# A graph-and-experts kernel: operands of the last diffusion step formed ahead, its last tiles written out apart, the expert pass unrolled

## The chip, the core and the metric

One core of one Trainium2 chip runs the whole program. The metric is the device time of one execution in microseconds (us). The kernel before takes 1402.74 us (median of 3 runs, 1402.63 to 1402.93).

## The reference

The input is `x` (3125 x 256, float32) and a graph with 103,125 directed edges. The part that matters:

```python
h = silu(layernorm(x) @ W_in.T + b_in)          # 3125 x 256
term = out = h
for i in range(1, 7):                           # 6 diffusion steps
    term = segment_sum(term[src], dst) * inv_deg[:, None] / i
    out = out + term
x = x + out @ W_out.T + b_out
xn = layernorm(x) * gamma + beta                # second part: 8 experts, top 2
top_vals, top_idx = top_k(xn @ Wr + br, 2);  w = softmax(top_vals)
y = sum over e of w_e * (gelu(xn @ W1[e] + b1[e]) @ W2[e] + b2[e])   # W1[e] 256 x 512, W2[e] 512 x 256
x = x + y
```

## The kernel before, in words

The 3125 nodes are 25 tiles of 125 rows (T = 25, D = 256), in 5 groups of 5 (WIN = 5, NB = 5). The graph is held in SBUF as dense fp16 counts (`adj`, 25 x 25 blocks of 125 x 125). Since W_out is linear, it is applied first: `h_dram` holds silu(...) @ W_out.T, and each of the 6 steps forms `v = h + (adj v) * cinv` (a nested form of the sum). A vector is carried as two fp16 parts side by side (512 columns), in `v_a` and `v_b` by turns, so that a tile of a step is 25 matmuls of 125 x 512 into one PSUM bank.

Building `adj` and the first step take until about 330 us. **Steps 1 to 4** (`step`, 25 tiles each) follow. For each tile TensorE (L1552) makes the product; ScalarE (L750) evicts the high half to `t_hi`; VectorE adds the low half (L993, `psum_read`), adds the row of `h` that SyncE has put into the two-deep `h_ring` (L1000, `h_used`), splits the sum into high and low fp16 and stores them (L1009, L1011, `v_ready`). Five PSUM banks let TensorE run up to five tiles ahead of the eviction; a new step reads every tile of the last one. In groups 0 to 3 of each of these steps SyncE also loads one piece of the expert weights per tile (`w_piece`, 128 x 256, 64 pieces in all) and VectorE takes its largest absolute value (L1079).

**The last step** (`last_step` with a `body(i, u, has)` on every engine) runs one software pipeline: in the body of tile m stand, on VectorE, the router logits of tile m - 8, `x1 = v * scale + (x + b_out)` and the mean and variance of tile m - 1 (L1189 to L1195), once in five tiles the square roots of a group (`sd2`, `newton`), the second normalisation of tile m - 5 (L1212, L1215, `z_ok`), the low half of the expert input of tile m - 6 (L1220), and the eviction of tile m (L1235, L1242). GpSimd adds `b_out` to the loaded `x` rows (L637) and `beta` to the normalised rows (L640). ScalarE makes the high half of the expert input of tile m - 5 (L808), then evicts tile m (L813), then copies the transposed rows of tile m - 6 (L818). TensorE follows tile m with two transposes of tile m - 6 (L1608) and the router matmuls of tile m - 7 (L1617). It has three PSUM banks in a ring for the product. Groups 0 and 1 are written out, 2 to 4 are a loop, and two more written-out groups (`peeled(NB)`, `peeled(NB + 1)`) drain the pipeline. After tile 4 stand the power-of-two scales (`scales`), which need the weights' maxima through two all-reduces on GpSimd.

As the last step frees groups of `adj`, 16 weight matrices of 512 KB are loaded into them from ScalarE's queue (`PART_RAW`), multiplied by their scale and split into a high fp16 part by ScalarE (L797) and a low one by VectorE (L1230), one in each of the bodies u = 1 to 4 of i = 1 to 4.

**Then** VectorE makes the routing (top 2, positions, tile tables; L1252 to L1385) and **the expert pass** runs over FT = 56 tiles of 128 rows (`ffn_tiles`): GpSimd gathers the rows (L661) and scatters the results (L667), TensorE transposes the rows of tile j + 2 (L1643), multiplies tile j by W1 (L1658) and tile j - 3 by W2 (L1675), ScalarE does gelu (L854), VectorE the rest (L1396, L1405, L1407, L1415). It is 7 groups of FU = 8 tiles, the first and last written out, five in a loop; at the start of a group each engine loads the 8 table values that its instructions need as addresses (which expert, which part of `adj`): TensorE 2 such loads, VectorE 3, ScalarE 1 (L375). The combination of the two results per row and the store end the program.

## Time and profile before

| | us |
|---|---|
| median of 3 runs | 1402.74 |
| the profiled execution, its own time | 1399.97 |
| its span, first to last instruction | 1398.2 |
| TensorE busy (mean granted clock 0.927) | 1199.9 |
| VectorE busy | 744.3 |
| ScalarE busy | 364.5 |
| GpSimd busy | 167.7 |

Start and duration of instructions are in us from the start of the span. A clock of 1.00 is TensorE's full speed. Names such as L1598 are lines of the kernel before.

### The profile page before, as it was taken

The page shows a single profiled execution, that of the slowest core. Times are in us where ns is not written, and L with a number is a line of the kernel's source. Part 1 is how long each engine was busy: PE and PEld are TensorE (multiplying, and loading weights), DVE is VectorE, ACT ScalarE, POOL GpSimd, SP SyncE. Part 2 cuts the span into 40 slices and gives each one's busy share as a digit, 9 for nine tenths or more (in the row PEclk, how much of TensorE's full clock was granted, in tenths as well). Part 3 has the DMA queues.
Part 4 walks back from the last instruction along what each step waited for, and adds up shares of the span by engine and source line. Part 5 has one row for each costly group of instructions (what it writes and reads, how often), then busy time and mean ns, then how long its engine had stood idle before and what let it go on. Part 6 is the DMA issues. An engine that isn't in the chain of part 4 may idle for free.

```text
span 1398.2 us, 28001 instructions
## 1 busy us (share of the span) xinstructions
PE 1199.9 (86%) x7796; PEld 836.1 (60%) x7797; DVE 744.3 (53%) x1521; ACT 364.5 (26%) x706; POOL 167.7 (12%) x193
## 2 busy tenths in 40 slices
PE   4896999999999999999999999988885468778860
PEld 2784776665666666666666665545453357667750
DVE  7588999963333333333333333366566744554445
ACT  0574656640000000000000000022213223433423
POOL 2000000000000000000000000111111134555440
PEclk8897999999999999999999999999987579989995
DMA  5110010022111111111101110233332012112119
GB/s 155 30 52 19 23 38 29 29 84 57 41 44 37 38 40 45 33 35 44 46 27 45 41 46 22 51 106 102 101 109 76 17 50 65 62 61 64 58 45 269
DMA packets 65272, 81.72 MB, mean 58 GB/s; under 512 B 10997, under 2 KB 55981, under 8 KB 65085
## 3 DMA queue, kind: packets, MB, share of 16 engines
q1 hardware_dynamic: 49126, 49.55, 12.4%
q10 hardware_dynamic: 9908, 16.37, 4.2%
q0 software_dynamic: 6176, 15.01, 3.5%
q8 instruction: 35, 0.57, 0.2%
q14 instruction: 27, 0.22, 0.0%
HBM read 62.34 MB, written 19.50 MB: 59 GB/s over the span
## 4 chain that ended last, share of the span: by engine, by line
PE 63%; DVE 11%; DMA 9%; issue 8%; DVEq 3%; ACT 2%; POOL 1%; another core or an unknown queue 1%; ACTq 1%; SPq 0%; POOLq 0%
PE ps L1552 39%; PE ps L1530 7%; PE ps L1498 4%; PE ps L1658 3%; PE ps L1675 3%; DVE v_b L986 2%; DMA adj<-L_ffn_W 2%; DMA v_b<-xs_dram,v_a 2%; PE ps L1466 2%; DMA adj<-y_dram 2%; PE ps L1598 2%; PE ps L1477 1%; DMA v_a<-x 1%; DVEq L375 1%
## 5 line engine op out<-in xcount | busy, mean ns | idle before, releaser
L1552 PE MATMUL ps<-v_a,adj 125*125 125x512 f16 x1375 | 297.3, 379 | 0.0
L1552 PE MATMUL ps<-v_b,adj 125*125 125x512 f16 x1250 | 270.2, 379 | 2.2 <-DVE v_b L1011 2.2
L1552 PEld LDWEIGHTS ps<-v_a,adj 125*125 (+1 forms) x1375 | 187.6, 136 | 109.0
L1552 PEld LDWEIGHTS ps<-v_b,adj 125*125 x1250 | 170.6, 136 | 101.6 <-issue 2.6
L993 DVE SCALAR_TENSOR_TENSOR t_hi<-ps,cinv,t_hi 125x256 f32<-125x256 f32 x125 | 60.3, 482 | 284.2 <-ACT t_hi L750 284.2
L750 ACT ACTIVATE t_hi<-ps,cinv 125x256 f32<-125x256 f32 x125 | 59.4, 475 | 526.0 <-PE ps L1552 496.3
L986 DVE TENSOR_TENSOR v_b<-v_b 125x2560 f16<-125x2560 f16 x125 | 180.3, 1485 | 7.1 <-PE ps L1498 6.5
L1598 PE MATMUL ps<-v_b,adj 125*125 125x512 f16 x625 | 153.6, 409 | 5.5 <-DVEq L1128 3.4
L1675 PE MATMUL ps<-adj,v_b 128*128 x672 | 115.3, 283 | 25.5 <-issue 19.0
L727 ACT ACTIVATE adj<-ps 125x625 f32 (+1 forms) x125 | 111.8, 906 | 75.1 <-PE ps L1498 74.3
L1598 PEld LDWEIGHTS ps<-v_b,adj 125*125 (+1 forms) x625 | 90.5, 147 | 61.5 <-issue 13.1
L1658 PE MATMUL ps<-v_b,adj 128*128 128x128 f16 x1344 | 119.7, 228 | 5.6 <-issue 4.9
L854 ACT ACTIVATE v_b<-ps,v_a 128x128 f32<-128x128 f32 x224 | 84.2, 457 | 150.6 <-PE ps L1658 101.0
L1530 PE MATMUL ps<-v_a,adj 125*125 125x512 f16 x500 | 123.4, 380 | 0.0
L1498 PE MATMUL ps<-v_b 125*128 125x125 f16 x1250 | 95.8, 225 | 17.0 <-issue 9.4
L1498 PEld LDWEIGHTS ps<-v_b 125*128 125x128 f16 x1250 | 82.9, 100 | 42.1 <-DVE v_b L986 16.2
L1658 PEld LDWEIGHTS ps<-v_b,adj 128*128 x1344 | 97.9, 102 | 13.2 <-issue 7.1
L618 POOL MEMSET v_a<- 128x128 f32 x1 | 0.2, 205 | 843.9 <-DVEq L1128 843.9
L1000 DVE SCALAR_TENSOR_TENSOR t_hi<-h_ring,scale,t_hi 125x256 f32<-125x256 f32 x125 | 60.6, 484 | 33.4 <-issue 17.4
L1675 PEld LDWEIGHTS ps<-adj,v_b 128*128 128x128 f16 x672 | 57.4, 101 | 33.9 <-issue 27.6
L1530 PEld LDWEIGHTS ps<-v_a,adj 125*125 (+1 forms) x500 | 60.9, 136 | 25.6 <-issue 0.6
L667 POOL DMA_INDIRECT y_dram<-adj,v_a x56 | 57.7, 1030 | 103.5 <-DVE adj L1415 82.9
(230 smaller groups left out, 940.1 us busy)
## 6 DMA issues: line engine op xcount, KB each, us to landing
h_ring<-h_dram SPq DMA_DIRECT2D x150, 125.0 KB
w_piece<-L_ffn_W SPq DMA_DIRECT2D x64, 128.0 KB, 2.1
adj<-L_ffn_W ACTq DMA_DIRECT2D x16, 512.0 KB, 6.1
v_a<-x SPq DMA_DIRECT2D x25, 125.0 KB
xs_dram<-v_a SPq DMA_DIRECT2D x25, 125.0 KB
adj<-x ACTq DMA_DIRECT2D x5, 560.0 KB
adj<-y_dram SPq DMA_DIRECT2D x5, 560.0 KB
adj<-y_dram ACTq DMA_DIRECT2D x5, 560.0 KB
```

The costliest lines, as they stand in the source:

```text
L727: a.activation(adj_w[:, row, :, bass.ds(T * i + WIN * u, WIN)].rearrange("b o q p -> b (o q) p"), cells.rearrange("b c q -> b q c"), ACT.C ...
L750: a.activation(t_hi[0:NP, :], ps[0:NP, bank, 0:D], ACT.Copy, scale=cinv[0:NP, s, bass.ds(WIN * i + u, 1)]).then_inc(S["hi_ok"], 1)
L854: last = a.activation(h_g[r][:, b * 128:(b + 1) * 128], ps[:, 2 + r, b * 128:(b + 1) * 128], ACT.Gelu, bias=b1T[:, bass.ds(e * HK + b, 1)] ...
L986: v.tensor_tensor(one_hot_bq[RB[u]], iota_x[:, None, :, :].broadcast_to(pairs), mine[:, :, None, :].broadcast_to(pairs), ALU.is_equal).the ...
L993: v.scalar_tensor_tensor(t_hi[0:NP, :], ps[0:NP, bank, D:2 * D], cinv[0:NP, s, bass.ds(t, 1)], t_hi[0:NP, :], ALU.mult, ALU.add).then_inc( ...
L1000: v.scalar_tensor_tensor(t_hi[0:NP, :], h_ring[0:NP, u % 2, :], scale[0:NP, 0:1], t_hi[0:NP, :], ALU.mult, ALU.add).then_inc(S["h_used"], 1)
L1498: last = te.matmul(cells[:, j * 128:j * 128 + Q], one_hot_bq[RB[u]][:, j, :, k], one_hot_bq[RB[u]][:, WIN + j, 0:Q, k], start=(k == 0), st ...
L1530: last = te.matmul(ps[0:NP, early_bank(w), :], of_tile(adj[0:NP, 0:ADJ], r - 1, w, a * NP, NP), va[:, a, :], start=(a == 0), stop=(a == T ...
L1552: last = te.matmul(ps[0:NP, u, :], of_tile(adj[0:NP, 0:ADJ], i, u, a * NP, NP), source[:, a, :], start=(a == 0), stop=(a == T - 1))
L1598: last = te.matmul(ps[0:NP, RB[u], :], of_tile(adj[0:NP, 0:ADJ], i, u, a * NP, NP), vb[:, a, :], start=(a == 0), stop=(a == T - 1))
L1658: last = te.matmul(ps[:, 2 + r, b * 128:(b + 1) * 128], w_block(part1, low, at, 128), xT16[u % XR][:, part * DK + k, :], start=(n == 0 and ...
L1675: last = te.matmul(ps[:, 4 + r, 0:D], hp[u % FR][:, b, :], w_block(part2, low, b * D, D), start=(b == 0 and n == 0), stop=(b == HK - 1 and ...
```

## The change

- **Rows.** A new tensor `hx_dram` holds h + x + b_out. GpSimd writes it after the reduction of the weights' maxima: a DRAM-to-DRAM copy of `h_dram`, an accumulating DMA of `x`, and one of `b_out` broadcast over 3125 rows, each waited for (3.2 MB each). The last step loads its ring rows from it, and its second VectorE operation writes `x1` directly. The 25 loads of `x`, the GpSimd additions of `b_out` and the extra `x1` operation are gone.
- **Weights.** Steps 1 and 2 take the maxima over 32 halves of 128 x 512 (16 a step, in the part of the destination vector that tiles 20 to 24 will fill). After step 2 GpSimd reduces them and VectorE forms the scales. Steps 3 and 4 load each half again, ScalarE makes the high part, VectorE the low part, and SyncE stores both to `w16_dram`. The last step only loads the finished 512 KB per matrix, on SyncE's queue.
- **Order.** The square roots of tiles 0 to 3, 4 to 8, ..., 19 to 23 are taken at u = 4; tile 24 has its own. `xn2` and `xs_r` have five buffers instead of three, the transposed rows and their PSUM banks two instead of one. `peeled(NB)` and `peeled(NB + 1)` are replaced by a written-out piece on each engine.
- **Expert pass.** `ffn_tiles` is written out over all 56 tiles. Each engine loads one value per table and tile, for the next tile: TensorE 1 (`part_of`; the layer is now in a static base address), VectorE 2, ScalarE 1.

```diff
...
+            pool.wait_ge(S["w_top_ok"], 1)
+            g.partition_all_reduce(w_all, w_top, 128, bass.bass_isa.ReduceOp.max).then_inc(S["w_all_ok"], 1)
...
+            g.dma_start(hx_dram, h_dram).then_inc(S["hx_ok"], 16)
+            pool.wait_ge(S["hx_ok"], 16)
+            g.dma_start(hx_dram, x, max_dma_last_dim=8192, accum_op=ALU.add).then_inc(S["hx_ok"], 16)
+            pool.wait_ge(S["hx_ok"], 32)
+            g.dma_start(hx_dram, bass.AP(b_out.tensor, 0, [[0, N], [1, D]]), accum_op=ALU.add).then_inc(S["hx_ok"], 16)
...
             def step(s, t0, t1):
+                raw, lo16 = w_spare(step_dest(s))
+                if s > 0:
+                    sp.wait_ge(S["tile_ps"], s * T)
+
+                def store(i, u):
+
+                    sp.wait_ge(S["piece_used"], (s - 1) * NE // 2 * WP + i * WP + (u + 3))
+                    sp.dma_start(w16_half(s, i, u, 0), w_hi16[:, :]).then_inc(S["w16_out"], 16)
+                    sp.dma_start(w16_half(s, i, u, 1), lo16).then_inc(S["w16_out"], 16)
...
+                        if pieces and s > 2 and u < WP:
+
+                            act.wait_ge(piece_in[u % 2], 16 * ((s - 1) * NE + (u // 2 + 1)) + 32 * i)
+                            act.wait_ge(S["w16_out"], 32 * (i * WP + u + 1) + 32 * NE * 2 * (s - 3))
+                            a.activation(w_hi16[:, :], raw[u % 2], ACT.Copy,
+                                         scale=sw[:, bass.ds((s - 3) * NE + 2 * i + u // 2, 1)]).then_inc(S["piece_hi"], 1)
...
+                                dve.wait_ge(S["piece_hi"], count - NE * 2 * 2 + 1)
+                                v.scalar_tensor_tensor(lo16, raw[u % 2], sw[:, bass.ds((s - 3) * NE + 2 * i + u // 2, 1)],
+                                                       w_hi16[:, :], ALU.mult, ALU.subtract).then_inc(S["piece_used"], 1)
...
-            peeled(NB)
-            peeled(NB + 1)
...
+            last = T - 1
+            statistics2(last)
+            v.tensor_copy(rows(mv2, last), mv_t)
+            v.tensor_scalar(ve3, mv_t[:, 1:2], 1 + 1e-5, 1e-5 ** 2, ALU.mult, ALU.add)
+            v.drain().then_inc(S["ve_ok"], 1)
+            for w in range(last - 4, last):
+                normalise2(w, w % WIN, rr[:, w:w + 1])
+                if w == last - 3:
+                    dve.wait_ge(S["sd_ok"], NB + 1)
+                    newton(v, sd3, ve3, rt3)
+                if w >= last - 2:
+                    low_rows(w - 3, (w - 3) % WIN)
+                if w >= last - 3:
+                    logits(w - 4, twin(w - 4, 0))
+            normalise2(last, last % WIN, sd3)
+            for w in range(last - 3, last + 1):
+                low_rows(w, w % WIN)
+                logits(w - 1, twin(w - 1, 0))
+            logits(last, twin(last, 0))
...
+def ffn_tiles(eng, count, unroll, lag, tables, steps, transposed, hidden, result):
+
+
+    entries = {0: [load(0, eng) for load in tables]}
+    transposed(0)
+    transposed(1)
+    for j in range(count + lag):
+        for b in range(steps):
+            if j >= lag:
+                result(j - lag, b, *entries[j - lag], alone=j >= count)
+            if b == 0 and j + 2 < count:
+                transposed(j + 2)
+            if j < count:
+                hidden(j, b, *entries[j])
+            if b == 0 and j + 1 < count:
+                entries[j + 1] = [load(j + 1, eng) for load in tables]
+        entries.pop(j - lag, None)
...
```

## Rows read from the trace of the kernel before

**Rows 1.** Windows: span, busy us (instructions) by engine, PEclk, DMA share, GB/s.

```profile
...
735.00:870.00 135.00, 135.00 (x627) 85.28 (x625) 48.90 (x116) 11.87 (x25) 0.00 (x0) 1.00 0.14 40
965.00:1010.00 45.00, 38.31 (x171) 23.30 (x169) 26.95 (x63) 13.15 (x25) 7.10 (x10) 0.92 0.34 107
1090.00:1125.00 35.00, 13.48 (x64) 9.71 (x62) 24.48 (x88) 7.19 (x10) 2.47 (x4) 0.50 0.02 5
1125.00:1360.00 235.00, 186.82 (x2240) 164.37 (x2240) 113.29 (x224) 84.25 (x224) 114.90 (x111) 0.93 0.19 59
...
```

**Rows 2.** Waits: engine, line, releaser, total us, times, longest us.

```profile
...
ACT adj L797 <- DMA adj<-L_ffn_W: 67.2, 12, 7.3
...
```

**Rows 3.** Groups: line, engine, operation, shape, count, busy us, mean ns, idle before.

```profile
...
L1230 DVE SCALAR_TENSOR_TENSOR adj<-adj,v_a (+1 forms) x16 | 22.3, 1397 | 24.6 <-ACT adj L797 24.5
...
```

**Rows 4.** Timeline of the last step, tiles 15 and 16: start, duration, engine, line.

```profile
...
992.56 0.43 DVE L1191 BATCH_NORM_STATS2 v_a<-adj 125x6 f32 x1
...
997.23 0.43 DVE L1215 TENSOR_TENSOR v_a<-v_a 125x256 f32<-125x256 f32 x1
...
999.71 0.48 DVE L1235 SCALAR_TENSOR_TENSOR t_hi<-ps,cinv,t_hi 125x256 f32<-125x256 f32 x1 [1.66 <-ACT t_hi L813]
...
1001.33 0.48 DVE L1189 SCALAR_TENSOR_TENSOR adj<-v_a,scale 125x256 f32 x1
...
1001.90 0.43 DVE L1191 BATCH_NORM_STATS2 v_a<-adj 125x6 f32 x1
...
1003.91 0.88 DVE L1215 TENSOR_TENSOR v_a<-v_a 125x256 f32<-125x256 f32 x1
...
```

**Rows 5.** Timeline, TensorE, two tiles of the last step.

```profile
...
930.10 5.59 PE L1598 MATMUL ps<-v_b,adj 125*125 125x512 f16 x25
...
936.47 5.59 PE L1598 MATMUL ps<-v_b,adj 125*125 125x512 f16 x25
...
```

**Rows 6.** Timeline after tile 4 of the last step: GpSimd, then VectorE.

```profile
...
916.77 0.62 POOL L637 TENSOR_TENSOR v_a<-v_a 125x256 f32<-125x256 f32 x1 [8.52 <-issue]
...
920.85 0.48 DVE L1235 SCALAR_TENSOR_TENSOR t_hi<-ps,cinv,t_hi 125x256 f32<-125x256 f32 x1 [1.65 <-ACT t_hi L813]
...
```

**Rows 7.** Timeline from the last tile's eviction to the last logits.

```profile
...
1073.82 0.48 DVE L1235 SCALAR_TENSOR_TENSOR t_hi<-ps,cinv,t_hi 125x256 f32<-125x256 f32 x1
...
1079.40 0.43 DVE L1215 TENSOR_TENSOR v_a<-v_a 125x256 f32<-125x256 f32 x1
...
1087.06 0.43 DVE L1215 TENSOR_TENSOR v_a<-v_a 125x256 f32<-125x256 f32 x1
...
1092.56 0.17 DVE L1181 TENSOR_TENSOR v_a<-ps,v_a 125x8 f32<-125x8 f32 x1 [1.37 <-PE ps L1617]
...
```

**Rows 8.** Timeline, TensorE, transposes of expert tiles 2, 19, 20, 25, 55.

```profile
...
1130.52 0.58 PE L1643 MATMUL ps<-v_a,v_b 128*128 128x128 f16 x4 [2.20 <-issue]
...
1197.97 0.39 PE L1643 MATMUL ps<-v_a,v_b 128*128 128x128 f16 x4
...
1200.85 0.39 PE L1643 MATMUL ps<-v_a,v_b 128*128 128x128 f16 x4
...
1218.38 0.40 PE L1643 MATMUL ps<-v_a,v_b 128*128 128x128 f16 x4 [0.94 <-DMA v_b<-xs_dram,v_a]
...
1342.00 0.40 PE L1643 MATMUL ps<-v_a,v_b 128*128 128x128 f16 x4 [1.33 <-DMA v_b<-xs_dram,v_a]
...
```

**Rows 9.** Line L375, table loads: ns min/median/max, first and last start.

```profile
...
L375 PEldq TENSOR_LOAD <-adj x15: 590/1007/2171, 1127.7 to 1350.5; - x15
...
L375 ACTq TENSOR_LOAD <-adj x7: 547/561/754, 1124.3 to 1321.8; - x7
...
```

**Rows 10.** Waits from 300 to 335 us: total us, times, longest.

```profile
...
DVE t_hi L1000 <- DMA h_ring<-h_dram: 13.4, 1, 13.4
...
PE ps L1552 <- DVE v_b L1011: 2.2, 1, 2.2
...
```

**Rows 11.** DMA issues: destination, source, queue, count, KB each.

```profile
...
v_b<-early_dram SPq DMA_DIRECT2D x1, 2240.0 KB
...
```

More of the change, by code:

```diff
@@ L53, in gnn_ffn @@
     LAG = 3
-    LEAD = 4
     assert FT % FU == 0
@@ L856, in tile @@
                 last.then_inc(S["gelu_ok"], 1)
-            def group(i):
-                es = experts(i, act, 0, FU)
-                for u in range(FU):
-                    tile(i, u, es[u])
-            group(0)
-            with act.Fori(1, FT // FU) as i:
-                group(i)
+            e = experts(0, act)
+            for j in range(FT):
+                e_next = experts(j + 1, act) if j + 1 < FT else None
+                tile(j, e)
+                e = e_next
             for r in range(FR):
@@ L1679, in result @@
                     last.then_inc(S["ffn_y"], 1)
[L1680 to L1710 removed]
+            ffn_tiles(pe, FT, FU, LAG, (parts,), HK, transposed, hidden, result)
+def ffn_tiles(eng, count, unroll, lag, tables, steps, transposed, hidden, result):
[13 more added lines that the diff above has]
+        entries.pop(j - lag, None)
 def newton(v, r, var, tmp):
```

467 lines of the change are left out of this document (241 added, 226 removed).

## The prediction

> **What bounds the kernel now.** I read the windows first, then the waits, then the timeline where the bound changes. The windows [rows 1] give four different limits. In steps 1 to 4 TensorE is busy 135.00 of 135.00 us at clock 1.00 while VectorE has work for 85: TensorE is the limit, a tile costs 135/25 = 5.40 us, and VectorE has 86 us free a step. In the last step (965 to 1010) TensorE is busy 38.31 of 45 and no engine is full. From 1090 to 1125 nothing is full and the clock is 0.50: a chain of small operations. In the expert pass TensorE is busy 186.82 of 235.
>
> In the last step tile 5 is evicted at 920.85 [rows 6] and tile 24 at 1073.82 [rows 7]: 152.97 us for 19 tiles, 8.05 each, against 5.40 in the steps before. Two things hold it there. One is the weights: ScalarE waits 67.2 us in total for the matrices to land [rows 2], in front of its own evictions, and VectorE's low half takes 1.40 us, 16 times [rows 3]. The other is a loop of dependences that goes once round per tile: normalise, GpSimd adds beta, ScalarE makes the high part and then evicts the next tile, VectorE adds, then statistics, then normalise again. A tile without a weight unit shows its length: the gamma multiplication L1215 starts at 997.23 and the next at 1003.91 [rows 4], 6.68 us. TensorE's own need per tile with transposes and router matmuls is 936.47 - 930.10 = 6.37 us at most [rows 5].
>
> In the expert pass the transposes of tile 2 start at 1130.52 and those of tile 55 at 1342.00 [rows 8]: 53 periods of 3.99 us. Two neighbours deep in a group are 1200.85 - 1197.97 = 2.88 us apart, six periods inside one group take 1218.38 - 1197.97 = 20.41 us, 3.40 each, and the rest is the group starts, where TensorE loads 16 table values, up to 2.17 us a load [rows 9].
>
> **The last step without weights and x rows.** The weight units leave the step: no ScalarE wait, no L797, no L1230. The `x1` operation L1189 leaves VectorE's loop too: it and its gap are 1001.90 - 1001.33 = 0.57 us [rows 4]. The loop becomes 6.68 - 0.57 = 6.11 us; all the rest of it (L1215, GpSimd, L808, L813, L1235, L1242, logits, statistics, L1212) stays, and five buffers or two PSUM banks do not shorten it, because each normalisation still waits for the eviction of the body before. TensorE at up to 6.37 is a near second limit; 6.1 is taken, with 6.4 as the other end (19 x 0.3 = 6 us more). The square roots come once in five tiles: L1191 to L1215 takes 997.23 - 992.56 = 4.67 us with them and 1003.91 - 1001.90 = 2.01 without [rows 4], so 2.66 more, four times after tile 5.
>
> Where it starts: after tile 4 the scales and all-reduces run. Removing one all-reduce and the weights' share of the scales makes VectorE earlier, but GpSimd's next instruction starts only at 916.77, 8.52 us after its reduction, waiting for nothing the profile shows [rows 6]; one reduction stays there. I take that stall as staying. Tile 5's eviction comes about 1.9 us after GpSimd starts on beta (L1215 to L1235 is 2.48 us, of which the gamma operation is 0.43 [rows 4]): 918.7, against 920.85. Then 19 x 6.1 + 4 x 2.66 = 126.5, so tile 24 is evicted at 1045.2 instead of 1073.82: **28.6 us less**.
>
> **The last tiles.** From the last eviction to the last logits are 1092.56 - 1073.82 = 18.74 us [rows 7]: 5.58 to the first of the five normalisations, 7.66 for the next four (1.92 each, one round of a single buffer), 5.50 from the last of them to its logits. With five row buffers and two transposed buffers the normalisations follow at VectorE's pace: 5.0 to the first (the 0.57 is gone), about 5.5 for four (0.95 each for L1212, L1215 and gaps, and some 1.7 of low rows and logits between), and some 3.7 for the last chain through GpSimd, TensorE, ScalarE, TensorE, VectorE. Those last two are estimates from the same rows; the ends are nothing saved and 7.7. I take 14.2, **4.5 us less**. The routing that follows is unchanged.
>
> **SyncE's queue in the last step.** It now carries the 512 KB of a matrix, a ring row of 125 KB and a store of 125 KB per tile. The bytes are fewer than before (no x rows), 762 KB in 6.1 us is about 125 GB/s against the 107 the window shows [rows 1]. A ring row is wanted one loop after it is issued, 5 to 6 us. I cost this at nothing; if the row lands late it delays L1242 and with it every later term of the loop.
>
> **Steps 1 to 4.** What is added per tile: SyncE loads 256 KB instead of 128 and, in steps 3 and 4, stores 256 KB; ScalarE and VectorE work on 128 x 512. All of it lies under TensorE's 5.40 us a tile: VectorE has 135 - 85.28 = 49 us free even by busy time plus gaps, and 16 operations of at most 1 us more fit. The queue waits form a second loop: the store of piece k must land before ScalarE writes piece k + 1. Two stores, a high part and a low part should take about 5 us, less than 5.40; and in the fifth tile of each group there is no piece. A delay does not reach TensorE until the evictions are five tiles late. The trace has such a case: a ring row queued behind the reload of 2240 KB (and 260 KB more) [rows 11] made VectorE wait 13.4 us, and TensorE lost 2.2 us [rows 10]. Before step 3 VectorE and ScalarE wait for the reduction and the scales, a few us, inside the same cover. Steps: 0, other end below.
>
> The new DRAM copies (3 x 3.2 MB) start after step 2 and have 270 us until SyncE waits for them. At the rate of the case just named (2.5 MB in 13.4 us, 187 GB/s) they take 17 us each, 51 together. Hidden, unless they starve the pieces (second rival).
>
> **The expert pass.** The group starts vanish; each tile gets one TENSOR_LOAD on TensorE and ScalarE and two on VectorE. No row shows a load of one value. The shortest load of eight is 547 ns on ScalarE and 590 on TensorE [rows 9]; the longest 2171. Since 590 is reached with eight values I take 0.55 for one, of which some 0.2 lies under the instructions already queued: 0.35 per tile. Below: nothing shows. Above: all 0.55. The period inside a group is 3.40, 0.52 above the undisturbed 2.88 [rows 8]; half of that I put down to catching up after group starts, so 2.88 + 0.27 + 0.35 = 3.50. VectorE with two loads needs about 2.1 of work and 1.1 of loads, 3.2, just below. 53 x (3.99 - 3.50) = 26.0 us. The ramp gains about 1, since the loads at 1128 are shorter. **27 us less**; ends 3.20 (42) and 3.40 + 0.55 = 3.95 (2).
>
> By the Trainium skill, "Runtime: NRT & Kernel Launch", section on instruction fetch, a register load costs about 200 ns per register. By that a one-value load would vanish under the queued instructions and the period would be 3.15, 45 us less instead of 27. The trace speaks against it in so far as loads of eight take 547 ns at best, not 1600; no row has one value.
>
> **Sum.** 28.6 + 4.5 + 27 = 60.1 us. The profiled execution takes 1399.97, so the changed one would take 1339.9; the median of the runs is 2.77 above the profiled one, so **1342.6**.
>
> **Rivals.**
> - *Loads hidden*: the loads cost nothing on TensorE, and GpSimd's stall after tile 4 goes. Period 3.15: 18.5 less; the stall about 3 less. 1321. For it: 547 ns for eight. Against: VectorE's two loads. 0.15.
> - *The copies take the queues' bandwidth*: the copies run beside step 3's pieces. If a tile's chain of ring row, store and piece takes 8 us while they run, and they run 85 us, VectorE falls 2.6 x 10 = 26 us behind, less the cover of about 20: TensorE loses 5 to 35. 1348 to 1378. For it: no cover exists for more than five tiles. Against: 2.5 MB cost only 2.2 us [rows 10]. 0.12. The Trainium skill ("DMA: Bandwidth & Descriptors", section "Queues, rings and completion order") says that each engine takes turns between its queues packet by packet; by that the ring row would be slowed and not blocked, which belongs to the small end of this case.
> - *Loads eat the gain*: 0.55 exposed on top of 3.40, 3.95 a period. 1342.6 + 24 = 1367. Against: the group starts' loads were longer in sum. 0.16.
> - *Slower*: the same place, another size. The store of a piece must land before the next, so with an accumulating copy holding each engine, a piece takes far longer than a tile. If the three copies need T us and TensorE nearly stands while they run, it loses about T - 25. It cancels 60 us when T passes 85, that is when the two accumulating copies run at half the 187 GB/s and pieces stop meanwhile; at T = 110, 1402.7 - 60 + 85 = 1428. 0.05.
> - *The change does not do what it says* (the loop of the last step is limited by something that did not leave, 8.05 stays): only the tail and the expert pass, 1371. Against: 6.68 in the tile without a weight unit. 0.03.
>
> **Chances and range.** My case, 0.49, by itself 1330 to 1355. 0.8 is held by 1318 to 1372. The measurement can tell about 0.2% (2.8 us) from no change. Faster 0.94, same 0.01, slower 0.05.
>
> **What would show it.** Steps: TensorE busy 135 of 135 in step 3 as well. Last step: evictions 6.1 apart and 8.8 at the square roots; no wait for a weight matrix on ScalarE. From the last eviction to the last logits 14 us. Expert pass: transposes 3.5 apart without group starts. Wrong if step 3 shows TensorE idle, if ring rows land late behind the 512 KB loads, or if VectorE's two loads set the expert period.

## The result, and the profile after

The changed kernel takes 1384.27 us (median of 4 runs, 1382.79 to 1386.19) against 1402.68 for the kernel before on the same chip: a ratio of 0.9872, 95% interval 0.9855 to 0.9889. It is faster by 18 us, 1.3 per cent and clear of the interval; forecast were 60, and the time is outside the range of 1318 to 1372. The profiled execution took 1385.32 us, its span 1383.5.

Cut at the same landmarks, the two spans differ like this (start of the instruction named, in us):

| stretch | before | after | difference | forecast |
|---|---|---|---|---|
| start to first product of the last step | 873.68 | 914.14 | +40.5 | 0 |
| to eviction of tile 5 | 47.17 | 45.58 | -1.6 | -2.1 |
| tile 5 to tile 24 | 152.97 | 121.02 | -31.9 | -26.5 |
| tile 24 to last logits | 18.74 | 14.87 | -3.9 | -4.5 |
| last logits to transposes of expert tile 2 | 37.96 | 36.46 | -1.5 | -1 |
| expert tile 2 to 55 | 211.48 | 194.41 | -17.1 | -26 |
| to the end | 56.20 | 57.02 | +0.8 | 0 |

Without that first line the change gains 55.2 us, of 60.1 forecast. The rest is one stretch. The windows of the changed kernel (columns as in [rows 1]) show it:

```profile
...
600.00:735.00 135.00, 100.05 (x440) 61.94 (x439) 36.57 (x84) 15.58 (x29) 4.57 (x4) 0.86 0.64 133
735.00:870.00 135.00, 135.00 (x627) 85.40 (x626) 57.08 (x123) 24.98 (x44) 0.00 (x0) 1.00 0.31 96
1010.00:1055.00 45.00, 42.26 (x213) 27.43 (x213) 22.25 (x71) 8.29 (x23) 6.26 (x7) 1.00 0.31 90
1125.00:1360.00 235.00, 188.90 (x2240) 158.31 (x2240) 121.55 (x242) 86.98 (x231) 116.99 (x112) 0.93 0.26 75
...
```

Step 4 (735 to 870) is full, as [rows 1] was and as forecast. Step 3 has 100.05 us of TensorE in 135, at a clock of 0.86, with the DMA engines busy 64 per cent. TensorE's work there, with the two gaps in brackets:

```profile
...
600.34 59.52 PE L1647 MATMUL ps<-v_b,adj 125*125 125x512 f16 x275
...
679.93 7.89 PE L1647 MATMUL ps<-v_b,adj 125*125 125x512 f16 x25 [20.07 <-DVE t_hi L1066]
...
702.71 57.65 PE L1647 MATMUL ps<-v_b,adj 125*125 125x512 f16 x253 [14.89 <-DVE t_hi L1066]
...
```

The gaps are 35.0 of the 40.5 us. The rest is the granted clock after them, 0.71 from 680 to 688 and 0.69 from 702.7 to 712, between TensorE's two levels of 1.2 and 2.4 GHz: 25 products take 7.89 us after the first gap, and 253 take 57.65 after the second, where at the pace before the gaps (59.52 for 275) they take 5.41 and 54.8; together 5.4 more. The waits of that stretch name what TensorE lacked:

```profile
...
ACT w_hi L856 <- DMA w_dram<-v_a: 66.2, 9, 21.8
...
DVE t_hi L1073 <- DMA h_ring<-h_dram: 35.0, 3, 28.2
PE ps L1647 <- DVE t_hi L1066: 35.0, 2, 20.1
ACT w_hi L856 <- DMA v_a<-L_ffn_W: 34.8, 3, 31.5
...
```

Read upwards from TensorE: it waited 35.0 us for VectorE to free PSUM (L1066), VectorE stood 35.0 us at a ring row of `h` (L1073, once for 28.2 us) and behind ScalarE, and ScalarE stood for the landing of a piece's store (up to 21.8 us) and of a piece's load (31.5 us once). The median of the 32 loads of 256 KB is 3.5 us. What else moved is in the page's list of DMA issues (last number: us from issue to landing):

```profile
...
hx_dram<-h_dram POOLq DMA_DIRECT2D x1, 3125.0 KB, 13.0
hx_dram<-x POOLq DMA_DIRECT2D x1, 3125.0 KB, 20.3
hx_dram<-L_gnn_b_out POOLq DMA_DIRECT2D x1, 3125.0 KB, 63.6
```

Three transfers of the same size, costed at 17 us each, took 13.0, 20.3 and 63.6 us. They began at 605.5, 618.8 and 639.4, and from 660 to 680 TensorE has 0.07 us of work.

The last step and its tail, to set against [rows 6, 7] (start, duration, engine, line; VectorE's operation on PSUM for tile 5, then for tile 24, then the last logits):

```profile
...
959.72 0.48 DVE L1319 SCALAR_TENSOR_TENSOR t_hi<-ps,cinv,t_hi 125x256 f32<-125x256 f32 x1 [5.90 <-ACT t_hi L887]
...
1080.74 0.48 DVE L1319 SCALAR_TENSOR_TENSOR t_hi<-ps,cinv,t_hi 125x256 f32<-125x256 f32 x1 [1.63 <-ACT t_hi L887]
...
1095.61 0.17 DVE L1268 TENSOR_TENSOR v_a<-ps,v_a 125x8 f32<-125x8 f32 x1 [0.67 <-PE ps L1718]
...
```

And the expert pass, to set against [rows 8, 9] (transposes of tiles 2 and 55; then the table loads, ns min/median/max):

```profile
...
1132.07 0.61 PE L1747 MATMUL ps<-v_a,v_b 128*128 128x128 f16 x4 [0.55 <-DMA v_b<-xs_dram,v_a]
...
1326.48 0.40 PE L1747 MATMUL ps<-v_a,v_b 128*128 128x128 f16 x4
...
L381 DVEq TENSOR_LOAD <-adj x112: 300/309/514, 1127.0 to 1335.7; - x112
L381 ACTq TENSOR_LOAD <-adj x56: 273/278/507, 1127.0 to 1330.2; - x56
L381 PEldq TENSOR_LOAD <-adj x56: 296/303/547, 1127.0 to 1330.2; - x56
...
```

A load of one value takes 0.30 us (0.28 on ScalarE), not 0.55.

### The profile page after: what moved, and what is told of

Read it like the earlier page. It is cut to its first block, busy times and chain, and to the rows that moved or that the text cites. A ratio compares the mean times of both kernels' runs of the same rounds, so it can differ in the third digit from the quotient of the medians.

```text
span 1383.5 us, 27811 instructions
## 1 busy us (share of the span) xinstructions
PE 1192.7 (86%) x7796; PEld 826.7 (60%) x7796; DVE 728.0 (53%) x1480; ACT 368.1 (27%) x722; POOL 158.1 (11%) x171
## 4 chain that ended last, share of the span: by engine, by line
PE 66%; DMA 10%; issue 9%; DVE 8%; ACT 2%; POOL 2%; DVEq 1%; another core or an unknown queue 1%; SPq 1%; ACTq 1%; POOLq 0%
PE ps L1647 35%; PE ps L1625 7%; PE ps L1777 5%; PE ps L1693 4%; PE ps L1761 4%; PE ps L1593 4%; DMA w_dram<-v_a 3%; DVE v_b L1059 3%; DMA v_a<-L_ffn_W 2%; DMA adj<-y_dram 2%; PE ps L1561 2%; PE ps L1572 1%; DMA v_b<-xs_dram,v_a 1%; DMA h_ring<-h_dram 1%
## 5 line engine op out<-in xcount | busy, mean ns | idle before, releaser
L1647 PE MATMUL ps<-v_b,adj 125*125 125x512 f16 x1250 | 275.7, 384 | 37.0 <-DVE t_hi L1066 35.0
L1066 DVE SCALAR_TENSOR_TENSOR t_hi<-ps,cinv,t_hi 125x256 f32<-125x256 f32 x125 | 60.2, 482 | 222.2 <-ACT t_hi L820 222.2
L1693 PE MATMUL ps<-v_b,adj 125*125 125x512 f16 x625 | 143.4, 389 | 5.1 <-DVEq L1234 3.3
L1761 PE MATMUL ps<-v_b,adj 128*128 128x128 f16 x1344 | 116.9, 222 | 6.5 <-issue 5.1
L1777 PE MATMUL ps<-adj,v_b 128*128 x672 | 112.4, 273 | 9.7 <-issue 7.2
L1693 PEld LDWEIGHTS ps<-v_b,adj 125*125 (+1 forms) x625 | 85.8, 140 | 55.3 <-issue 4.3
L1761 PEld LDWEIGHTS ps<-v_b,adj 128*128 x1344 | 94.0, 99 | 16.1 <-issue 9.5
L1073 DVE SCALAR_TENSOR_TENSOR t_hi<-h_ring,scale,t_hi 125x256 f32<-125x256 f32 x125 | 60.5, 484 | 71.2 <-DMA h_ring<-h_dram 51.4
L1777 PEld LDWEIGHTS ps<-adj,v_b 128*128 128x128 f16 x672 | 52.2, 97 | 23.9 <-issue 17.4
## 6 DMA issues: line engine op xcount, KB each, us to landing
hx_dram<-x POOLq DMA_DIRECT2D x1, 3125.0 KB, 20.3
hx_dram<-L_gnn_b_out POOLq DMA_DIRECT2D x1, 3125.0 KB, 63.6
```

Source lines behind the costliest of these rows:

```text
L1066: v.scalar_tensor_tensor(t_hi[0:NP, :], ps[0:NP, bank, D:2 * D], cinv[0:NP, s, bass.ds(t, 1)], t_hi[0:NP, :], ALU.mult, ALU.add).then_inc( ...
L1073: v.scalar_tensor_tensor(t_hi[0:NP, :], h_ring[0:NP, u % 2, :], scale[0:NP, 0:1], t_hi[0:NP, :], ALU.mult, ALU.add).then_inc(S["h_used"], 1)
L1647: last = te.matmul(ps[0:NP, u, :], of_tile(adj[0:NP, 0:ADJ], i, u, a * NP, NP), source[:, a, :], start=(a == 0), stop=(a == T - 1))
L1693: last = te.matmul(ps[0:NP, RB[u], :], of_tile(adj[0:NP, 0:ADJ], i, u, a * NP, NP), vb[:, a, :], start=(a == 0), stop=(a == T - 1))
L1761: last = te.matmul(ps[:, 2 + r, b * 128:(b + 1) * 128], w_block(home, 0, low, at, 128), xT16[u % XR][:, part * DK + k, :], start=(n == 0 a ...
L1777: last = te.matmul(ps[:, 4 + r, 0:D], hp[u % FR][:, b, :], w_block(part, 1, low, b * D, D), start=(b == 0 and n == 0), stop=(b == HK - 1 a ...
```

## The experiments

The chips that ran them differ: the kernel before took 1376 to 1379 us on four of them and 1410 on a fifth (e11, e12). Each is therefore given as its ratio to the kernel before on its own chip, and its stretches from its own profile. The changed kernel's first product of the last step stands at 914.1, and at 909.8 when it was profiled again (r_after); about 873.5 is what it would be with nothing lost. This landmark scatters: e5, e7 and e8 are the same program up to the last step, and their profiles have 889.7, 882.4 and 882.5, so a few us of it are no evidence.

| run | what it is | first product of last step | ratio, 95% interval |
|---|---|---|---|
| r_after | the changed kernel again | 909.8 | 0.9877, 0.9851 to 0.9903 |
| e1_no_bias | without the third transfer | 873.3 | 0.9604, 0.9588 to 0.9620 |
| e2_no_copies | without any | 875.0 | 0.9610, 0.9593 to 0.9626 |
| e3_early | all three at 305 us | 915.4 | 0.9866, 0.9833 to 0.9899 |
| e4_wide_bias | third from a 25-row copy of b_out | 903.0 | 0.9806, 0.9790 to 0.9823 |
| e5_spread | third in five parts | 889.7 | 0.9699, 0.9678 to 0.9720 |
| e6_x_rows | third adds single rows of x | 896.9 | 0.9761, 0.9737 to 0.9785 |
| e7_evict_first | e5, ScalarE evicts first | 882.4 | 0.9625, 0.9591 to 0.9658 |
| e8_no_tables | e5, no table loads | 882.5 | 0.9576, 0.9547 to 0.9605 |
| e9_bias_first | b_out filled in, then h, x added | 917.4 | 0.9926, 0.9904 to 0.9949 |
| e10_sum_ahead | fill and x at 30 us, e7 | 890.9 | 0.9619, 0.9602 to 0.9636 |
| e11_distinct | e9 with distinct source rows | 887.3 | 0.9621, 0.9604 to 0.9639 |
| e12_sum_windows | fill and x at 109 us, e7 | 897.2 | 0.9631, 0.9612 to 0.9650 |
| e13_doubled | fill by doubling, x, h apart, e7 | 873.8 | 0.9510, 0.9490 to 0.9529 |

### Is it the transfers, and which? (e1, e2)

```diff
-            pool.wait_ge(S["hx_ok"], 32)
-            g.dma_start(hx_dram, bass.AP(b_out.tensor, 0, [[0, N], [1, D]]), accum_op=ALU.add).then_inc(S["hx_ok"], 16)
```

> Only the third DRAM copy is left out, which adds b_out to hx_dram in rows of 1 KB, so the last step's rows lack b_out. Theory A (step 3 stalls because the three copies, 13.0 + 20.3 + 63.6 = 96.9 us in the changed kernel's profile, slow the loads and stores of weight pieces, and TensorE loses what is over its cover of five tiles): with 33 us of copies left, pieces fall some 15 us behind, inside the cover; TensorE loses 0 to 10 in step 3 instead of 35 to 40, time 1345 to 1356. Rival B (step 3 is slow for another reason: its first stores, the reduction for the scales, or the larger pieces): time stays at 1384, step 3 still loses 40. Rival C (the accumulation of x is what stalls it, since the first long waits, 16.45 us, fall in or just after it): 1365 to 1375.

> All three DRAM copies are left out and the last step reads h_dram; x and b_out are not added. Theory A (the copies alone make the 40 us): TensorE busy 135 of 135 in step 3 as in step 4, first matmul of the last step at 874 instead of 914, time 1344. Rival B (the pieces or the scales make it): 1384, or in between by what they cost by themselves. It also gives the base from which each copy is priced: e1 less e2 is the cost of the first two copies, the changed kernel less e1 that of the third.

Both give all of it back. Step 3 in e1, then in e2:

```profile
...
600.00:735.00 135.00, 135.00 (x627) 85.38 (x626) 54.30 (x123) 22.28 (x41) 2.12 (x3) 1.00 0.47 134
...
```

```profile
...
600.00:735.00 135.00, 135.00 (x627) 85.37 (x626) 55.29 (x123) 23.29 (x41) 0.39 (x1) 1.00 0.29 86
...
```

The last step starts 41 and 39 us earlier, and the two ratios are equal within their intervals. So the first two transfers, 33 us together beside the pieces, cost nothing, and the third costs everything. Rivals B and C fall. Theory A's 1345 to 1356 us are ratios of 0.959 to 0.967 to the 1402.7 that they were worked out from; measured are 0.9604 and 0.9610.

### Does another place help? (e3)

```diff
+            with pool.If(fast == 1):
+                (the waits for h_out and the three transfers)
             pool.wait_ge(S["w_top_ok"], 1)
```

> All three copies kept whole, but issued as soon as the h rows are stored and the coverage flag is known (about 340 us, in steps 0 and 1) instead of after the maxima of step 2; in steps 1 and 2 the pieces are only loaded and reduced, and nothing is stored. Theory A with the store in the loop (what hurts is the store of a piece, which must land before ScalarE writes the next): nothing is lost, 1344 to 1348. Rival D (the copies delay any load, so that the ring rows and piece loads of step 1 fall behind in the same way): the loss moves to step 1 and stays 20 to 40 us, 1365 to 1385.

The loss moved with the transfers (305 to 404 us, end of step 0 and start of step 1, where nothing is stored): TensorE has 36.2 us of work between 335 and 403, and the last step starts at 915.4. So the store of a piece is not what makes it. Between 300 and 410 VectorE waited 76.9 us for ring rows, in five waits of up to 29.6. Rival D is right.

### Is it the row size? (e4, e6)

```diff
+            g.dma_start(b25_dram, bass.AP(b_out.tensor, 0, [[0, 25], [1, D]])).then_inc(S["hx_ok"], 16)
...
-            g.dma_start(hx_dram, bass.AP(b_out.tensor, 0, [[0, N], [1, D]]), accum_op=ALU.add).then_inc(S["hx_ok"], 16)
+            g.dma_start(hx_dram.rearrange("(p e) f -> p (e f)", e=25), bass.AP(b25_dram.tensor, 0, [[0, N // 25], [1, 25 * D]]),
+                        max_dma_last_dim=8192, accum_op=ALU.add).then_inc(S["hx_ok"], 16)
```

> b_out is first copied into a DRAM buffer of 25 rows (25 KB), and the third copy adds that buffer to hx_dram in 125 rows of 25 KB instead of 3125 rows of 1 KB; same bytes, same place. Theory E (the third copy takes 63.6 us by the size of its rows): it takes about 20 us as the accumulation of x did, copies 54 + 2 us in all, TensorE loses 5 to 20 in step 3, time 1350 to 1365. Rival F (it takes 63.6 because it reads and adds over pieces of step 3, whatever its rows): still about 60 us, time 1384.

> The third copy adds x again, with its rows permuted, instead of b_out, so the last step's rows are wrong: same destination, same rows of 1 KB (3125, in four DMAs of 750 to 875 rows, each waited for), but every row read from an address of its own. Theory H (the 63.6 us come from reading one and the same address 3125 times): the four together take 20 to 30 us, step 3 loses 0 to 10, ratio 0.961 to 0.968. Rival P (an accumulation in packets of 1 KB is slow by its packets; e4 still had packets of about 2 KB and took 59.1): 60 to 70 us together, ratio about 0.985.

Neither tells what it was meant to. e4's transfer took 59.1 us, and three of e6's four began 25, 21 and 25 us apart, which looked like "rows do not matter" and "small packets are slow". But the DMA queues show another shape than was intended. GpSimd's queue while the third transfer runs, in e4 (packets, MB, share of 16 engines):

```profile
...
q0 software_dynamic: 1616, 3.21, 27.9%
...
```

27.9 per cent of 16 engines is 4.5: an access pattern with 125 rows outermost was worked by some five engines. The packet records of e4's trace agree: five packets were in flight for two thirds of the time, and hardly ever more, where `x` had 16. The mean packet of 2 KB is no packet at all: 500 of 6.4 KB carried the data, beside 1100 of 8 bytes. e6 has about the same share (27.3 per cent), and its data went in 3125 packets of 1 KB. The Trainium skill has the rule ("DMA: Bandwidth & Descriptors", section "Why a DMA increments its semaphore by 16 and not by 1"): the number of engines is the largest up to 16 that divides the outermost dimension, which for 125 is 5. The shares of both runs agree with it. It does not carry over to 3125 rows outermost, where it gives 5 again: the changed kernel's third transfer kept 54.7 per cent of 16 busy. So the 59.1 us of e4 are five engines at 11 GB/s each, which is what each of sixteen reached when `x` was added (3.2 MB in 20.3 us, 10 each), and they say nothing of reading one address over and over (the hot address).

### One address, or adding? (e9, e11)

```diff
-            g.dma_start(hx_dram, h_dram).then_inc(S["hx_ok"], 16)
+            g.dma_start(hx_dram, bass.AP(b_out.tensor, 0, [[0, N], [1, D]])).then_inc(S["hx_ok"], 16)        # e9
+            g.dma_start(hx_dram[0:2048, :], bass.AP(W1.tensor, 0, [[2 * D, 2048], [1, D]])).then_inc(S["hx_ok"], 16)   # e11
+            g.dma_start(hx_dram[2048:N, :], bass.AP(W1.tensor, D, [[2 * D, N - 2048], [1, D]])).then_inc(S["hx_ok"], 16)
             pool.wait_ge(...)
             g.dma_start(hx_dram, x, max_dma_last_dim=8192, accum_op=ALU.add).then_inc(S["hx_ok"], 16)
-            g.dma_start(hx_dram, bass.AP(b_out.tensor, 0, [[0, N], [1, D]]), accum_op=ALU.add).then_inc(S["hx_ok"], 16)
+            g.dma_start(hx_dram, h_dram, max_dma_last_dim=8192, accum_op=ALU.add).then_inc(S["hx_ok"], 16)
```

> The three transfers in the same place, in another order: hx_dram is first filled with b_out (3125 rows of 1 KB, no addition), then h is added, then x, both in the large packets that the second copy of the changed kernel has (415 packets, 20 us). Theory P (adding in small packets is what takes 60 us): the fill takes 13 to 25 us, the two additions 20 each, 55 to 65 in all; loss in step 3 0 to 15 us; ratio to before 0.961 to 0.972. Rival H (reading one address 3125 times is slow, adding or not): the fill alone takes 50 to 60 us, the three 90 to 100, ratio about 0.987.

> As e9, but the fill of hx_dram reads rows of 1 KB, each from an address of its own (the first half of 3125 rows of 2 KB of W1, so the last step's rows are wrong), instead of b_out 3125 times; 1 KB per packet and no addition in both. Theory H (one address read 3125 times is what is slow; e9's fill took 50.2 us against 13 for the copy of h): the fill takes 15 to 25 us, 55 to 65 for the three, loss in step 3 at most 12 us, ratio 0.961 to 0.970. Rival P2 (packets of 1 KB are slow, whatever they read): 45 to 55 us and the loss of e9 (42 us), ratio 0.99.

The pair decides for filling. Both fill 3125 rows of 1 KB without adding; e9 reads one row 3125 times, e11 reads 3125 different rows. In e9 the fill took

```profile
...
hx_dram<-L_gnn_b_out POOLq DMA_DIRECT2D x1, 3125.0 KB, 50.2
...
```

50.2 us. In e11 the two halves, in flight together, landed 11.2 and 14.0 us after their issues, both within 15 us of the first. The queues in the same 13 us of each (608 to 621; packets, MB, share of 16 engines; q0 is GpSimd's fill, q1 the loads and stores of SyncE), e9 first:

```profile
...
q0 software_dynamic: 214, 0.88, 77.1%
q1 hardware_dynamic: 31, 0.05, 1.3%
...
```

and e11:

```profile
...
q0 software_dynamic: 809, 3.18, 75.6%
q1 hardware_dynamic: 579, 0.68, 15.1%
...
```

Packets are of one size (4.1 and 3.9 KB) and the engines are as busy (0.77 and 0.76), but a packet takes 13 x 16 x 0.771 / 214 = 0.75 us from the one address and 13 x 16 x 0.756 / 809 = 0.19 us from distinct ones. And beside the first, SyncE's queue moved 0.05 MB where it moved 0.68 beside the second: one piece load took 42.9 us, one store 37.2. Filling from one address is slow, and it starves what runs beside it. The pair differs in one thing more, that e11's rows are of another tensor and come in two transfers at once; since the engines are as busy in e9 with its one, a second transfer is not what e9 lacked.

For the changed kernel's own third transfer, which adds, the pair says less. The packet records of the traces have 3125 packets of 1 KB each, all adding: 0.11 us in the mean from distinct rows, with 4.4 of 16 engines busy (e6), and from the one address 0.17 in the changed kernel, 0.14 in r_after and 0.21 in e3. So the address costs there too, but not four times, and part of the 63.6 us belongs to adding in small packets: 3125 packets of 0.11 us on 16 engines are 21 us by themselves. No run adds distinct rows of 1 KB on all engines, so the two shares stay open.

The Trainium skill says in the same page, section "Queues, rings and completion order", that an engine takes turns between its queues packet by packet. Two more windows of e9 show where the trace agrees and where it does not. From 609.4 to 628.2:

```profile
...
q0 software_dynamic: 317, 1.30, 83.4%
...
```

and from 632 to 652:

```profile
...
q0 software_dynamic: 330, 1.35, 78.8%
q1 hardware_dynamic: 330, 0.35, 6.0%
...
```

In the second, one packet of SyncE goes through for one of the fill, as the page says; and since the fill's are 4.1 KB at 0.75 us and SyncE's 1.1 KB, that is 0.35 MB in 20 us. In the first, none goes through in 19 us, although a ring row (issued at 608.9), the two stores of a piece (611 and 612) and a piece load (614.8) are under way. Why is not settled by any run here.

e9's ratio is worse than the changed kernel's (0.9926) though its three transfers take 90 us and not 97: perhaps because the slow one stands first and the 20 us ones follow before VectorE has caught up; no run tests that. e11 lost 14 us with 54 us of fast transfers beside the pieces, where e1 lost nothing with 33. So the limit lies between 33 and 54 us, above the 27 us that five tiles last: beside fast transfers the pieces are slowed and not stopped.

### Parts, and other places (e5, e10, e12)

```diff
+            for k in range(5):                                                                    # e5
+                pool.wait_ge(S["tile_ps"], 3 * T + 10 * k)
+                g.dma_start(hx_dram[625 * k:625 * k + 625, :], bass.AP(b_out.tensor, 0, [[0, 625], [1, D]]), accum_op=ALU.add).then_inc(S["hx_ok"], 16)
+                pool.wait_ge(S["hx_ok"], 48 + 16 * k)
```

> All three copies kept; the third (b_out, rows of 1 KB) is cut into five of 625 rows, each issued when TensorE has finished 10 more tiles (from the start of step 3 to tile 15 of step 4). Theory A2 (what costs is one uninterrupted stretch of 63.6 us, longer than the cover of five tiles, some 27 us): each part takes about 12.7 us, VectorE recovers between, TensorE busy 135 of 135 in steps 3 and 4, ratio to before 0.960 to 0.963 as without the third copy. Rival D2 (the delay per byte stays, whatever the cut): the loss stays near 38 us, ratio 0.987. In between: pieces fall behind by sum, 0.97 to 0.98.

> hx_dram is filled with b_out and x is added right after the edge gathers (about 30 us into the run, where the DMA engines are busy 11 to 16 per cent), and only h is added after the reduction of the weight maxima, one transfer of 20 us; ScalarE evicts before it makes the high part, as in e7. Theory (what costs is DMA time next to the pieces beyond 33 us; e1 had 33 and lost nothing): TensorE busy 135 of 135 in steps 1 to 4, ratio 0.950 to 0.955 (e1 or e2 0.961, less the 8 to 11 us of e7). Rival (the early transfers delay the loads of x or the stores of h rows, from which all starts): the first 150 us grow by 5 to 30 us, ratio 0.955 to 0.975.

> As e10 (fill with b_out, x added, h added after the reduction of step 2, ScalarE evicts first), but the first two wait until all rows of the first features are made (about 147 us), so that they run beside the window stage, in which the DMA engines are busy 16 per cent and x is loaded and the h rows stored. Theory: the 17 us that e10 lost in its first 150 us come back and nothing is lost elsewhere; first matmul of the last step at 873 to 876, ratio 0.950 to 0.955. Rival: the early rows' stores in the window stage wait behind the 50 us fill as the pieces do, and the window stage grows by 10 to 20 us; ratio 0.957 to 0.967.

None of the three came out as its theory had it. e5's ratio of 0.9699 lies at the edge of the case in between, and e10 and e12 are as their rivals said. e5's parts took 14.5 us each, not 12.7. The first two followed the addition of `x` closely (637.1 and 661.8), so that 73 us from the first transfer on had one break of 10; the third, at 718.7, fell on the last rows of step 3, and step 4 began with a gap of 4.4 us. 16 us were lost in all (9 in e7, the same but for the eviction). The last two parts, alone in step 4, cost nothing. In e10 the fill runs from 30 to 81 us, and the last step starts 17 us late. 14 of them fall before the first ring row is used (at 154.6, and at 140.4 in the changed kernel), where ScalarE waits 13.9 us for one store of an `h` row to land; TensorE's work between 70 and 150 falls from 66.1 to 58.5 us with the DMA share up from 0.11 to 0.43. e12's fill was meant to begin at about 147 us; it began at 109.1 and ran to 161, a stretch in which the DMA engines of the kernel before are busy 6 per cent. 24 us are lost, 21.2 of them at the first ring row:

```profile
...
DVE t_hi L1075 <- DMA h_ring<-h_dram: 21.2, 1, 21.2
...
```

A mean DMA share says nothing here: it is enough that one small load or store on the path stands behind the hot address.

### The last step: who sets 6.0 and 7.9? (e7)

```diff
-                if has(5):
-                    high_rows(m - 5, u, i - 1)
                 if has(0):
                     ...
                     a.activation(t_hi[0:NP, :], ps[0:NP, RB[u], 0:D], ACT.Copy, ...).then_inc(S["hi_ok"], 1)
+                if has(5):
+                    high_rows(m - 5, u, i - 1)
```

> e5 and, in the last step, ScalarE evicts tile m before it makes the high part of row m-5, instead of after. Theory (the loop normalise, beta, high part, eviction, addition, statistics, normalise sets the last step where the square roots are, and nearly elsewhere): broken, TensorE sets the period, 6.0 us for every tile and none of 8.0 at the square roots, tile 5 to 24 in 114 to 116 us instead of 121; 5 to 8 us less than e5. Rival (the period is TensorE's already, and the 8.0 at the square roots is VectorE's own chain with its waits for ScalarE's root): under 2 us less.

Tile 5 to 24 takes 113.8 us against 121.2 in e5. Two evictions around the square roots in e5, then in e7 (VectorE's operation on PSUM; the roots stand between the two of each pair):

```profile
...
1015.93 0.48 DVE L1322 SCALAR_TENSOR_TENSOR t_hi<-ps,cinv,t_hi 125x256 f32<-125x256 f32 x1 [1.63 <-ACT t_hi L890]
...
1023.87 0.48 DVE L1322 SCALAR_TENSOR_TENSOR t_hi<-ps,cinv,t_hi 125x256 f32<-125x256 f32 x1 [1.63 <-ACT t_hi L890]
...
```

```profile
...
1002.40 0.48 DVE L1322 SCALAR_TENSOR_TENSOR t_hi<-ps,cinv,t_hi 125x256 f32<-125x256 f32 x1 [1.61 <-ACT t_hi L888]
...
1008.62 0.48 DVE L1322 SCALAR_TENSOR_TENSOR t_hi<-ps,cinv,t_hi 125x256 f32<-125x256 f32 x1
...
```

7.94 us become 6.22, and a group of five takes 30.0 us, 6.00 a tile. All of it is TensorE's (e7):

```profile
...
960.00:1030.00 70.00, 70.00 (x362) 46.80 (x362) 38.28 (x121) 14.33 (x38) 9.88 (x11) 1.00 0.42 127
...
```

The loop that the prediction described is real; in the changed kernel it holds the square-root tiles and TensorE the others. The ratio is 0.9625 against 0.9699, about 10 us. In the profiles the last step is 10.8 us shorter, 3.4 of them before tile 5 and 7.4 after; the 7.3 us by which e7's starts earlier are scatter, since the edit is not in that part.

### The expert pass: what are the tables worth? (e8, r_before, r_after)

```diff
-    entries = {0: [load(0, eng) for load in tables]}
+    entries = {0: [0 for load in tables]}
```

> e5 and no table loads in the expert pass: every tile uses expert 0 and part 0, on all engines, so the expert outputs are wrong, while instructions, gathers and scatters stay. Theory L (the one-value loads, 0.30 us each, are exposed on TensorE or VectorE): period 3.67 becomes 3.2 to 3.4, 15 to 25 us less than e5. Rival G (GpSimd's gathers and scatters, 2.6 to 3.3 us a tile, or instruction fetch set it): period stays 3.6 to 3.67, under 4 us less.

> The kernel before, profiled on the same chip as the others of this call, to have both expert passes from one chip. e5 had 3.22 us a tile in the expert pass, the changed kernel's first profile 3.67, with the same instructions, and the times of before differ too (1376 to 1379 against 1403). If the chip makes the difference, the expert pass of before has here 3.5 to 3.6 us a tile instead of 3.99, the loop of its last step stays 8.05, and the rest stays within 0.5%.

> The changed kernel on the same chip. Expert pass 3.2 us a tile as in e5; 0.3 to 0.35 us less than before there, so 16 to 19 us; step 3 loses about 38 us to the third copy; ratio 0.985 to 0.989. If the expert pass shows 3.67 here, the difference between chips was not the reason, and the third copy or its place would be.

Without tables tiles 2 to 55 take 154.4 us, 2.91 each: the undisturbed 2.88 of [rows 8]. With them e5 takes 170.9, 3.22. The difference, 0.31 us, is the length of one load of one value (e8's addresses are static as well, which this does not separate). Theory L holds: the load is exposed whole.

On the chip of r_before and r_after the pass takes 1324.06 - 1133.13 = 190.93 us before (3.60 a tile) and 1298.82 - 1127.49 = 171.33 after (3.23), 19.6 less. So the 3.67 of the first profile belongs to its chip and not to the kernel: there both kernels take 21 and 23 us more in this pass, and e11 and e12, on the chip where the kernel before took 1410, have 195 and 198 us for it. Its waits name what is extra. Expert pass of the first profile:

```profile
...
ACT v_b L929 <- remote: 45.7, 8, 17.1
...
DVE adj L1510 <- remote: 23.8, 11, 2.7
...
PEld ps L1747 <- DMA v_b<-xs_dram,v_a: 7.4, 16, 0.8
...
```

r_after has no wait on "remote" in that pass and 1.2 us of PEld's for the gathers. The kernel before has them on the first chip (ScalarE 48.4 us, VectorE 31.6) and not on the other (r_before), so they are not the change's. What these waits are was not tried.

### Both repairs together (e13)

```diff
+            pool.wait_ge(S["tile_ps"], T + 3)
+            g.dma_start(hx_dram[0:NP, :], bass.AP(b_out.tensor, 0, [[0, NP], [1, D]])).then_inc(S["hx_ok"], 16)
+            done = NP
+            for k in range(5):
+                pool.wait_ge(S["hx_ok"], 16 + 16 * k)
+                more = min(done, N - done)
+                g.dma_start(hx_dram[done:done + more, :], hx_dram[0:more, :]).then_inc(S["hx_ok"], 16)
+                done += more
...
+            pool.wait_ge(S["tile_ps"], T + 15)
+            g.dma_start(hx_dram, x, max_dma_last_dim=8192, accum_op=ALU.add).then_inc(S["hx_ok"], 16)
...
+            g.dma_start(hx_dram, h_dram, max_dma_last_dim=8192, accum_op=ALU.add).then_inc(S["hx_ok"], 16)
```

> hx_dram is filled without a long read of one address: 125 rows from b_out, then five copies, each from the rows already filled (125, 250, 500, 1000, 1125 rows), starting when tile 28 is finished (early in step 1); x is added when tile 40 is finished, h after the reduction of step 2; ScalarE evicts first as in e7. Theory (bursts of up to 20 us of large packets lie inside the cover of five tiles, only the hot address does not): the six fills together take 20 to 35 us, TensorE busy 135 of 135 in steps 1 to 4, first matmul of the last step at 873 to 876, last step and evictions as in e7; ratio to before 0.950 to 0.956. Rival (the chain of copies delays the pieces as well, or copies from rows just written are slow too): 5 to 20 us are lost in step 1, ratio 0.958 to 0.968.

1309.85 us against 1378.24 before on its chip, a ratio of 0.951 (0.949 to 0.9529): 67 us less, where the changed kernel gains 17 to 18. The theory came out in every number. The six fills take 25 us (347.4 to 372), `x` 19.8 and `h` 21.7, and all four steps are full but for their start (the kernel before has 134.55 in the first of these windows). Doubling, the earlier place and the pause before `x` were changed together, so their shares are not told apart:

```profile
...
330.00:465.00 135.00, 134.32 (x623) 85.02 (x624) 53.24 (x117) 11.87 (x25) 4.24 (x7) 1.00 0.37 102
465.00:600.00 135.00, 135.00 (x627) 85.42 (x626) 53.19 (x116) 11.88 (x25) 0.00 (x0) 1.00 0.19 55
600.00:735.00 135.00, 135.00 (x628) 85.34 (x627) 54.59 (x123) 22.74 (x41) 1.43 (x2) 1.00 0.40 110
735.00:870.00 135.00, 135.00 (x627) 85.42 (x626) 54.26 (x116) 23.31 (x41) 0.00 (x0) 1.00 0.28 86
...
```

## Why the prediction was wrong

- **The DRAM copies (the step that failed).** "At the rate of the case just named (2.5 MB in 13.4 us, 187 GB/s) they take 17 us each, 51 together. Hidden, unless they starve the pieces". The rate came from a reload that reads each byte once (187 GB/s, [rows 10, 11]). It fits the copy of `h` (13.0 us) and the addition of `x` (20.3). It does not fit 3125 additions of the same 1 KB: 63.6 us, and "hidden" was wrong with it. The row used as the nearest neither read one address nor added in packets of 1 KB; e9 and e11 show what the first costs, and the second was not tried by itself. It cost 40.5 us; the other terms fell short by 60.1 - 55.2 = 4.9. That is 45.4 against the profiled execution, and 41.7 between the median and the forecast, since the profiled one of before lay 2.8 below its median and the one of after 1.1 above.
- **The rival was there, too cheap.** "The copies take the queues' bandwidth" had the mechanism, the cover of five tiles and 5 to 35 us, with a chance of 0.12; "slower" named the point: a total over 85 us with the pieces stopped. The total was 96.9 us. The rule of that rival, T - 25, gives a loss of 72 for it; measured are 40.5, because the pieces were slowed and not stopped, and in the first 33 us by less than the cover (e1). The sentence on turns in the prediction put the case at its small end; 19 us without one packet of SyncE (e9) speak against that. The argument against it, that 2.5 MB had cost only 2.2 us, priced one burst of 13 us; a burst shorter than the cover says nothing of a longer one. e1, e11 and e9 give the scale: 33 us of transfers cost 0, 54 cost 14, 90 to 97 with the hot address 36 to 44.
- **A misread column.** "VectorE has work for 85" and "135 - 85.28 = 49 us free" take the second column of [rows 1], TensorE's weight loads, for VectorE, whose 48.90 is the third. "86 us free" is right. The error was on the safe side and changed no term.
- **Steps 1, 2 and 4.** Right: 135.00 of 135 in step 4 with its pieces and stores; the reduction and scales before step 3 cost nothing (e1, e2 full).
- **The last step.** Right in kind, 31.9 us for tiles 5 to 24 against 26.5, and in part by luck. The quiet tiles come at 6.02 to 6.11 (forecast 6.1) and a group of five at 32.8 (forecast 33.2), but the 6.1 was worked out from the loop, and e7 shows that in a quiet tile TensorE sets 6.00; the two lie close together. Of the 5.5 us that were over, 3.1 are the start: the three tiles after tile 5 come at 5.03 to 5.10, not 6.1, since their products are made while the scales hold the evictions. Most of the rest is at the square roots, where the longest interval is 8.2 and not 8.8. GpSimd's stall after its reduction stayed, as assumed. e7 shows the loop by breaking it.
- **The tail.** Right in its sum, 14.87 us against 14.2, by errors that nearly cancel. From the last eviction to the first gamma multiplication are 3.1 us (forecast 5.0), to the fifth 7.0 more (5.5), and from there to the last logits 4.7 (3.7):

```profile
...
1083.86 0.43 DVE L1280 TENSOR_TENSOR v_a<-v_a 125x256 f32<-125x256 f32 x1
...
1090.87 0.43 DVE L1280 TENSOR_TENSOR v_a<-v_a 125x256 f32<-125x256 f32 x1
...
```

- **The expert pass.** The kind was right, two numbers were off. The load of one value was taken as 0.55 us with 0.35 exposed; it takes 0.30 and is exposed whole (e8: 0.31). The rest of the period was taken as 2.88 + 0.27; on the chips without the extra waits it is 2.91. So 3.50 was too high for those (3.23) and too low for the first (3.67). The gain, 17.1 us there and 19.6 on another chip against 26, is off because the forecast took the kernel before at 3.99 a tile; 0.39 of that is the chip's (3.60 on the other) and stays after the change. VectorE's two loads did not set the period.
- **SyncE's queue in the last step.** Costed at nothing, and right: no ring row is late there.
- **Loads hidden** and **loads eat the gain** were both wrong: the load is exposed whole, but it is 0.30 us and not 0.55. The period of 3.15, for a load that vanishes, was not seen (3.23 and 3.67).

## What to carry to other kernels

Before a transfer is costed by the rate of another, compare how the two read: a broadcast of one row out of DRAM is not a copy of as many bytes, and it slows the loads and stores beside it. Fill such a tensor by doubling, from rows already written: 25 us in e13, with nothing lost, against 50 to 52. And a cover is a length, not a share: transfers beside a pipeline that runs five tiles ahead were free up to 33 us in one piece here, and cost 14 us at 54 and about 40 at 90 to 97, so cut them with pauses in which the pipeline can catch up.

## What the runs showed of the hardware

- 3.2 MB from DRAM to DRAM on GpSimd's queue: 13 to 16 us copied, 19 to 24 us added in packets of 7.7 KB; 50 to 52 us filled from one address of 1 KB, 15 us from distinct addresses (e11); 59 to 64 us added from one address.
- Beside the fill from one address SyncE's queue moved 0.05 MB in 13 us, beside the other 0.68; later beside the same fill the two queues went packet for packet (330 and 330 in 20 us).
- Adding from the one address, in packets of 1 KB (changed kernel, 641 to 700, GpSimd's queue): 59 x 16 x 0.547 / 3108 = 0.17 us a packet, as slow per KB as e9's fill (0.75 us for 4.1 KB). From distinct rows adding takes 0.11 for such a packet (e6), and filling 0.05 per KB (e11).

```profile
...
q0 software_dynamic: 3108, 3.16, 54.7%
q1 hardware_dynamic: 1553, 1.81, 14.4%
...
```

- The two additions with 125 outermost (e4, e6) kept 4.4 and 4.5 of 16 DMA engines busy.
- While the engines are held, SyncE's own instruction that issues a DMA takes up to 4.4 us instead of 0.36, in step 3 of the changed kernel (3.2 in this stretch):

```profile
...
639.58 0.36 SPq L506 DMA_DIRECT2D w_dram<-w_hi  x1
...
644.26 3.17 SPq L507 DMA_DIRECT2D w_dram<-v_a  x1
...
```

- A table load of one value takes 0.28 to 0.31 us on TensorE, VectorE and ScalarE; eight values 0.55 at best [rows 9].
- The same program differs by 2 per cent between chips (1376.7 and 1402.7 us), nearly all of it in the pass with gathers and scatters (190.9 and 211.5).
